# Relative values through a bank of the transposes' ring; values and transposes nearer to the scores

## What is computed

```python
scores = jnp.einsum('bhqd,bhkd->bhqk', Q, K) / SCALE
rel_k = pek[idx]
scores = scores + jnp.einsum('bhqd,qkd->bhqk', Q, rel_k) / SCALE
scores = jnp.where(causal[None, None], scores, -jnp.inf)
attn = jax.nn.softmax(scores, axis=-1)
out = jnp.einsum('bhqk,bhkd->bhqd', attn, V)
rel_v = pev[idx]
out = out + jnp.einsum('bhqk,qkd->bhqd', attn, rel_v)
```

## Time and profile before

| | |
|---|---|
| median of 3 runs | 5536.34 us (5535.29 to 5539.28) |
| profiled execution | 5535.59 us, span 5533.9 us |
| PE busy | 5134.9 us (93%) |
| weight loads busy | 3347.5 us (60%) |
| DVE busy | 3774.5 us (68%) |
| ACT busy | 3425.3 us (62%) |
| POOL busy | 1831.3 us (33%) |
| DMA | 1418.07 MB, mean 256 GB/s |

### The profile page before, as it was taken

The page is one execution under the profiler, slowest core; times in us unless marked ns, Lnnn a source line. Parts: engine busy times, 40 slices in busy tenths (PEclk is TensorE's granted clock), DMA queues, the critical chain, the costliest instruction groups (busy, mean ns, idle before and its releaser), DMA issues. The chain is left out here.

```text
span 5533.9 us, 143122 instructions
## 1 busy us (share of the span) xinstructions
PE 5134.9 (93%) x49460; PEld 3347.5 (60%) x49460; DVE 3774.5 (68%) x8777; ACT 3425.3 (62%) x7512; POOL 1831.3 (33%) x2516
## 2 busy tenths in 40 slices
PE   9986999999999999999999999999999799999999
PEld 5554666666666666666666666666666455665665
DVE  5555777777777777777777777777777455555554
ACT  4445888878778887887877878778787211111111
POOL 3443333333333333333333333333333011111111
PEclk9997999999999999999999999999999899999999
DMA  7888999999999999999999999999999311111110
GB/s 223 254 252 264 329 323 324 332 316 323 321 324 324 325 323 321 324 328 325 322 325 327 322 321 327 316 323 327 324 322 304 99 61 56 50 61 61 61 55 32
DMA packets 654368, 1418.07 MB, mean 256 GB/s; under 512 B 64072, under 2 KB 362544, under 8 KB 641456
## 3 DMA queue, kind: packets, MB, share of 16 engines
q1 hardware_dynamic: 653744, 1409.89, 77.5%
HBM read 737.46 MB, written 672.14 MB: 255 GB/s over the span
## 5 line engine op out<-in xcount | busy, mean ns | idle before, releaser
L809 ACT ACTIVATE a_prob<-a_neg_s,a_neg_max 128x384 f32<-128x384 f32 (+1 forms) x1792 | 1081.1, 603 | 209.1 <-DVE a_neg_max L858 193.2
L524 DVE COPY a_p_t<-a_t_ps 128x512 f32<-128x512 f32 (+3 forms) x1536 | 952.5, 620 | 24.8 <-PE a_t_ps L773 23.9
L773 PE MATMUL a_t_ps<-a_ident,a_prob 128*128 128x128 f32 x5120 | 924.5, 280 | 31.5 <-DVE a_p_t L524 20.4
L858 DVE CUSTOM_DVE_ANT_1 a_neg_s<-a_s_ps,a_bias,a_far_neg 128x384 f32<-128x384 f32 x1280 | 791.0, 618 | 237.6 <-DVE a_far_neg L852 237.6
L706 PE MATMUL a_s_ps<-a_k,a_q 96*128 96x512 bf16 (+3 forms) x3072 | 852.7, 332 | 107.2 <-ACT a_far L813 105.1
L852 DVE TENSOR_REDUCE a_far_neg<-a_s_ps 128x1 f32<-128x640 f32 (+4 forms) x1280 | 708.8, 554 | 312.0 <-PE a_s_ps L706 178.5
L816 ACT ACTIVATE a_b_out<-a_t_ps 128x512 f32<-128x512 f32 (+1 forms) x1024 | 587.4, 574 | 384.4 <-PE a_t_ps L716 364.6
L734 PE MATMUL a_o_ps<-a_p_t,a_v 128*32 128x128 f32 x18432 | 782.0, 279 | 7.8 <-ACT a_o_t L821 0.2
L813 ACT ACTIVATE a_far<-a_s_ps,a_neg_max 128x640 f32<-128x640 f32 (+4 forms) x1280 | 730.6, 571 | 0.0
L816 ACT ACTIVATE a_p_t<-a_t_ps 128x512 f32<-128x512 f32 (+3 forms) x1536 | 672.8, 438 | 71.0 <-PE a_t_ps L773 53.4
L773 PE MATMUL a_t_ps<-a_ident,a_far 128*128 128x128 f32 x3840 | 662.5, 278 | 55.5 <-DVE a_p_t L524 52.2
(11 more groups left out here) (99 smaller groups left out, 6678.4 us busy)
## 6 DMA issues: line engine op xcount, KB each, us to landing
a_bias<-bias_scr SPq DMA_DIRECT2D x448, 576.0 KB, 7.8
prob_scr<-a_prob SPq DMA_DIRECT2D x448, 576.0 KB, 6.5
bias_scr<-a_b_out SPq DMA_DIRECT2D x448, 512.0 KB, 7.1
a_band<-prob_scr SPq DMA_DIRECT2D x448, 512.0 KB, 5.6
qk_scr<-p_parts SPq DMA_DIRECT2D x256, 192.0 KB, 3.4
v_scr<-p_v_out SPq DMA_DIRECT2D x256, 128.0 KB, 2.2
a_v<-v_scr SPq DMA_DIRECT2D x64, 512.0 KB, 8.9
attn_scr<-a_o_t SPq DMA_DIRECT2D x512, 64.0 KB, 7.4
```

The costliest lines, as they stand in the source:

```text
L524: copy(p_t[par][:, head, blocks[0] * P:(blocks[-1] + 1) * P], bank[:, 0:len(blocks) * P]) \
L773: mm = pe.transpose(bank[:, n * P:(n + 1) * P], prob_block(r, kk, head, b), ident[:, :])
L809: e = act.activation(near_prob(r, k, u, near(qb)), neg_s[:, u % 2, 0:w].rearrange("p (b c) -> p b c", c=P), ACT.Exp, bias=neg_max[:, u:u + ...
L858: dve.tensor_tensor_reduce(by_block(neg_s[:, u % 2, 0:w]), by_block(s_ps[:, u % 2, lo:lo + w]), near_bias(r, k, u, near(qb)), -1.0, begin, ...
```

## The change

The relative values no longer add to `o_ps`. They become a job of their own, `rel`, last in unit 0, and write a bank of the ring like a transpose. The product by values is closed in `o_ps` by itself; ACT copies it to `o_t` in unit 3 of the step in which it is made, and DVE later adds the ring's bank to that copy in place, signalling `o_sum`, for which SyncE's store waits. `o_t` has four slots for two. `VALUE_SLOTS` puts values of tile k-2 (was k-3) in step k, and `P_LAG` goes from 7 to 5: in step k the transposes are of head 3 of tile k-2 in unit 0 and heads 0 to 2 of tile k-1 in units 1 to 3. The relative values stay in unit 0 of step k for tile k-4.

```diff
+    OUT = 4
-        o_t = sb("a_o_t", [P, 2, P])
+        o_t = sb("a_o_t", [P, OUT, P])
+        o_sum = sem("a_o_sum")
-        P_LAG = 7
+        P_LAG = 5
         BAND_SLOTS = ((2, 3), (3, 3))
-        VALUE_SLOTS = ((1, 3), (2, 3), (3, 3))
+        VALUE_SLOTS = ((1, 2), (2, 2), (3, 2))
...
+                if u == REL_SLOT[0] and ok(k - REL_SLOT[1]) and k >= 0:
+                    jobs.append(("rel", u, k - REL_SLOT[1], 0, None))
...
-            if kind == "band":
+            if kind == "rel":
+                eng.wait_ge(o_sum, TILES * r + kk + 1)
+            elif kind == "band":
...
+                if kind == "rel" and name == "dve":
+                    eng.wait_ge(o_mm, TILES * r + kk + 1)
+                    eng.wait_ge(o_evac, TILES * r + kk + 1)
+                    eng.tensor_tensor(o_t[:, kk % OUT], o_t[:, kk % OUT], bank[:, 0:P], ALU.add).then_inc(o_sum, 1)
...
-                        sp.wait_ge(o_evac, T - 3)
+                        sp.wait_ge(o_sum, T - 3)
-                        sp.dma_start(row[g, :, qb * P:(qb + 1) * P], o_t[:, par]).then_inc(stored[par], 16)
+                        sp.dma_start(row[g, :, qb * P:(qb + 1) * P], o_t[:, (k - 4) % OUT]).then_inc(stored[par], 16)
...
-                                       p_t[par][:, h, j * P:(j + 1) * P], start=(j == 0), stop=False)
+                                       p_t[par][:, h, j * P:(j + 1) * P], start=(j == 0), stop=(j == qb))
...
-            def relative(r, k):
+            def relative(r, k, bank):
-                for n in range(first_j(q_block(k)) // P, 2):
+                n_first = first_j(q_block(k)) // P
+                for n in range(n_first, 2):
-                        mm = pe.matmul(o_ps[h * VW:(h + 1) * VW, 0:P], pv[:, n], band_t[:, par, h, n * P:(n + 1) * P],
-                                       start=False, stop=(n == 1))
+                        mm = pe.matmul(bank[h * VW:(h + 1) * VW, 0:P], pv[:, n], band_t[:, par, h, n * P:(n + 1) * P],
+                                       start=(n == n_first), stop=(n == 1))
...
+                            elif kind == "rel":
+                                relative(r, kk, bank)
-                        if u == REL_SLOT[0] and ok(k - 4) and k >= 0:
-                            relative(r, k - 4)
...
-                        if u == REL_SLOT[0] and ok(k - 4) and k >= 0:
-                            act.wait_ge(o_mm, T - 3)
+                        if u == VALUE_SLOTS[-1][0] and ok(k - 2) and k >= 0:
+                            act.wait_ge(pv_mm, T - 1)
-                            act.activation(o_t[:, k % 2], o_ps[:, 0:P], ACT.Copy).then_inc(o_evac, 1)
+                            act.activation(o_t[:, (k - 2) % OUT], o_ps[:, 0:P], ACT.Copy).then_inc(o_evac, 1)
```

## The result

The changed kernel takes 5572.19 us (median of 4 runs, 5568.49 to 5573.38) against 5536.53 us, a ratio of 1.0063 (95% interval 1.0045 to 1.008). The forecast was 5484. The profiled execution took 5572.41 us (span 5570.7).

What follows compares the result with a forecast made beforehand. Even steps were taken as DVE's, odd as PE's, transfers close behind. From 59.75 us a cycle, -2.0 even, +0.7 odd and 0.9 for transfers gave 59.35 against 60.18: 52 us less over 64 cycles, 5484 us; range 5440 to 5550.

Steps and rivals of the forecast that it cites:

- What bounds the kernel: Attention stage: even steps DVE's, odd steps PE's, transfers close behind; engines alone need 59.75 us a cycle, transfers cost 0.43.
- The turn at o_ps: PE's wait for ACT's copy of o_ps: removing it is worth nothing, and the new copy in unit 3 costs nothing.
- The add: 512 new DVE operations, 0.25 us each (bounds 0.20 and 0.29), 2.0 us a cycle; on DVE's own chain in even steps.
- Even steps, -2.0 us: Steps 0, 2, 4, 6 of a cycle shorten as DVE loses large copies: -0.75, -0.15, -0.48, -0.62 us.
- Odd steps, +0.7 us: Steps 1, 3, 5, 7 of a cycle: step 1 grows 0.5 us, the others 0.2 together from coupling and ring edges.
- The ring: At step edges: four more edges a cycle hand over a bank used two jobs before, each costing 0 to 0.3 us.
- The transfers: DMA in the attention stage: holds on the engines rise from 0.43 to 0.9 us a cycle, taking back part of the gain.
- The rivals: Transfers take nearly all, 5533, chance 0.19; whole gain kept, 5453 or 5427, 0.16; odd steps become DVE's, 5610 or 5677, 0.13.
- the slow rival: Odd steps become DVE's, its copies on the path as PE and DVE take turns: 5610 or 5677 us, chance 0.13.

Runs made afterwards that it cites:

- before_ring_on: The kernel before, with the ring's place running on from one step to the next, nothing else changed: 5531.89 us, 0.9996.
- own_columns_unshifted: own_columns with the shift undone (values three steps behind, transposes seven units behind) and ACT's copy of o_ps a step later: 5558.13 us, 1.0044.
- own_columns: after_ring_on with the relative values written to free columns of o_ps's own bank, no rel job in the ring: 5518.22 us, 0.9979.
- after_ring_on: The changed kernel with the ring's place running on over steps, each bank handed over three jobs later: 5563.36 us, 1.0058.
- after: The changed kernel itself, as measured against the kernel before: 5572.19 us, 1.0063.
- own_columns_early_copy: own_columns with ACT's copy of o_ps put first in unit 3, ahead of its other copies: 5515.1 us, 0.9967.
- shifted_empty_place: own_columns without DVE's add and PE's wait for it, plus an empty ring place in unit 0 of each step: 5554.27 us, 1.0035.

## Why the prediction was wrong

**The account.** From the kernel before (5532 beside these runs), by medians: the add, its two turns and ACT's moved copy +26 us, the shift -40, the ring job +45, the step edges +9, together +40 for the 36 measured. The terms are differences between neighbouring kernels, so they add up by construction. The same chain in the traces, us a cycle, mean of the same 48 cycles:

```
                         even    odd
before_ring_on          29.83  30.28
own_columns_unshifted   30.31  30.18   the add, its turns, ACT's moved copy
own_columns             29.20  30.61   the shift
after_ring_on           29.26  31.40   the ring job
after                   29.21  31.51   the step edges
```

*What bounds the kernel.* Right in kind: 59.75 us of the engines' own time was the base, and the new one, 60.51 by the medians of the units, stands as firmly.

*The turn at o_ps.* Right that PE waits for no copy there: no such wait is among the rows after. But I asked only whether the new copy is done in time, and priced it at nothing. On ACT it now lies ahead of unit 0's copies, where it delays PE by 0.16 to 0.17 us in three units 1 (about 30 us of the time with a ring place and without the shift; with the shift its share isn't separated).

*The add.* Right in duration, 283 ns between the bounds of 0.20 and 0.29 us, and beside PE's scores in odd steps. DVE's busy time in the whole program rose by 137 us, within the 100 to 150 foretold. Of the add's 2.0 us a cycle little is on the path: 7 to 15 us of time, and not the 64 that its 0.25 us in each even step made.

*Even steps, -2.0 us: the first step that failed.* They gave 0.66: 0.34, 0.24 and 0.24 in steps 0, 4 and 6, where 0.75, 0.48 and 0.62 were forecast, and step 2 grew by 0.15 where I had it shrink by as much. I let DVE's sum fall and kept DVE as the bound. By the marks of the table DVE's busy time in even steps fell by 1.57 us a cycle, not 2.2, and its idle time rose by 0.92. Of that, 0.58 is a wait for PE's transposes in unit 3, where it had none; the rest isn't assigned. (The larger part of the rise from 15.0 to 100.9 us in that wait lies in odd steps.) A sum of one engine's work gives the gain only until the next engine is reached, and I allowed for that in step 2 alone. The shift as a whole gave 36 to 43 us with the add in place, and 25 between the two kernels that free the bank at once (5582.61 to 5557.79), where the same terms promised over 80 before the transfers took their part.

*Odd steps, +0.7 us.* They took 1.21. Step 1, priced at +0.5, grew by 0.14; steps 3, 5 and 7, priced at 0.2 together, grew by 1.07. The coupling was expected, its place and size were not.

*The ring: the step that decided.* I counted the ring's jobs at the step edges only and priced four edges at up to 0.3 us. Both kernels with edges mended show that the edges are worth 0 and 3 to 9 us. What I had no term for is the extra place inside the step: it brings PE back to ACT's two banks of unit 0 one job early, 0.2 to 0.3 us for each, and costs 45 to 51 us (21 us as an empty place in the kernel before). It turned a gain of 0.2% (own_columns) into a loss of 0.6%.

*The transfers.* I let them take back 0.5 us a cycle. They took nothing, since nothing was gained; in own_columns_early_copy they do hold the engines again. A step of the changed kernel moved 393 GB/s, as one before moved 394. Whether the figure of 358 GB/s (the Trainium skill, DMA: Bandwidth & Descriptors, Specifications) or the share of 0.97 is the limit, no run here tried.

*The rivals.* Odd steps, already 0.43 us a cycle longer than even ones, are 2.3 us longer now, but they are not DVE's: the slow rival had the sign and not the mechanism. DVE is idle for 8.4 of their 31.5 us. PE's loads wait 2.2 us a cycle for DVE in them (1.6 before) and 4.7 for ACT (2.4 before); with the edges mended it is 1.2 for DVE and 6.0 for ACT.

## What to carry to other kernels

In a ring of few buffers filled in a fixed order, a new user can cost even if it takes no time and frees its buffer at once, because the filler meets the older users sooner; count for each unit whose buffer the next job reuses and how long ago that one was filled. An operation moved off one engine's wait may land ahead of another's urgent work; look at what it now precedes. Spare columns of a bank whose users already wait for each other can be cheaper than a place in the ring. And a sum by the bounding engine holds only down to the next engine's order, so write down for each step which engine is next and how near.

## What was not expected of the hardware

The attention stage is all but a clockwork where no transfer holds it: over 48 cycles of the kernel before, half of the 32 units spread by less than 0.005 us (standard deviation), while units that wait for transfers spread by up to 0.24. One place in a ring shows up in shifted_empty_place as waits of 0.21 and 0.27 us in the same unit of step 5, in all 48 cycles, at a granted clock of 1.00. An engine busy 79% of the time (ACT, 2376.43 of 3000 us) was the one that was waited for.
